# GpSimd's 512-column two-input operations issued as two of 256 columns in a two-layer transformer kernel

## The chip, the cores and the metric

The kernel runs on one core of a Trainium2 chip. The metric is the device time of one execution in microseconds; less is better. The core has five engines with a queue each: TensorE (PE, its weight loads shown as PEld), VectorE (DVE), ScalarE (ACT), GpSimd (POOL) and SyncE (SP), which here issues all DMAs.

## The reference

Two layers of a pre-norm transformer, B = 8 sequences of T = 1024 tokens, D = 256 features, 16 heads of 16. Each layer is attention and a feed-forward part, both on a layer norm of the input and both added to it:

```
x = x + L0_attn(layernorm(x))      # softmax(q k^T / 4, causal) v, then w_out
x = x + L0_ffn(layernorm(x))       # gates by entmax-1.5 over 16 experts; factorised experts with gelu
x = x + L1_attn(layernorm(x))      # low-rank q, k, v; half of each head's q and k rotated:
                                   #   x * cos + rot(x) * sin
x = x + L1_ffn(layernorm(x))       # squared-relu shared expert, and a top-2 router whose
                                   # truncated weights are 0 unless one logit dominates
```

## The kernel before

The work is cut into chunks: a sequence b, a half c of its tokens (512, one PSUM bank of columns), a layer l. An attention **pass** is (b, l, c), 32 in all; a **unit** is one of four groups of four heads in a pass. A planner written in Python (`Plan`, `program_order`) runs once before the code is emitted and gives one list, `ORDER`. Every engine walks through that list and emits its own share of each item, in order, so the order on each engine's queue is fixed and the engines meet only at semaphores.

What each item is on which engine, as far as the change matters:

- **Projection** (`qk`): TensorE makes 128 rows by 512 tokens of q or k, ScalarE copies them to a `scratch` buffer in float32 (L1581).
- In layer 1 these are **rotated**: VectorE swaps neighbouring rows (`swap_pairs`, L1865, a stream shuffle from scratch to scratch), GpSimd multiplies the original by the cosine table (`times_cos`, L1761), the swapped copy by the sine table (L1782) and adds the two (L1785, both in `rotate`).
- **Splitting**: q and k are stored as two float16 parts. ScalarE makes the first (`parts` slot 0, L1588 in layer 1, L1580 in layer 0), GpSimd subtracts it from the float32 value and so makes the second (`part2`, L1767). SyncE stores both to DRAM (L1057, L1058) and later loads them as the stacked operands `stk_q`, `stk_k` of the units (`load_stack`, L1073, L1075).
- **Scores**: TensorE makes score tiles (L1282), VectorE takes their row maxima out of PSUM (L1877 with the causal mask, L1880 without; L1885 joins the maxima of two halves), GpSimd splits the maxima into float16 parts (L1797 to L1799). TensorE makes the scores again, transposed, with the maximum subtracted (L1321); ScalarE writes the exponentials to `probs` (L1616); GpSimd zeroes what lies above the diagonal (`causal`, L1777); TensorE weighs the values (L1340).
- **Division**: the outputs of a unit go through DRAM; VectorE inverts the sums (L1889), SyncE stores and reloads the inverses, spread over rows (L1102, L1107), and GpSimd multiplies (`divide`, L1806). TensorE's output projection follows (L1259).
- **Layer norm**: VectorE takes statistics of each of 4 tiles of 128 tokens (`statistics`, L1844, L1850, L1852, L1853), GpSimd raises the variance to -1/2 and makes the shift (L1751, L1753), ScalarE normalises. The raw statistics of 4 tiles lie in a buffer `st6` with two slots: one for the first norm of layer 0 (n = 0), one for the three others.
- **Entmax and router**: long chains of small VectorE operations on 128 x 4 to 128 x 128 values in SBUF (L1913 to L1966 and L1976 to L1994), each waiting for the one before. GpSimd takes two powers for them (L1825, L1828).

In the four places of GpSimd's code that rotate, split and divide, each operation reads two operands of 128 rows by 512 columns and writes one, and its semaphore is raised at its end.

## Time and profile before

| | us |
|---|---|
| median of three runs | 2695.77 |
| lowest, highest | 2695.38, 2698.12 |
| the profiled execution | 2700.38 |
| its span in the trace | 2698.4 |
| TensorE busy in it | 2440.8 |
| VectorE busy | 2042.8 |
| ScalarE busy | 1869.6 |
| GpSimd busy | 1031.5 |

The span is from the first to the last instruction; some 2 us lie around it. All rows below come from the one profiled execution. Matmuls overlap in the array, and their ends are modelled, so TensorE's busy time is an upper reading. A row of a group gives the mean duration of one instruction and the idle time of the engine just before them with what ended it; a row of the timeline gives the start, the length and, in brackets, the idle time before.

### The profile page before, as it was taken

What the parts mean: (1) busy time and instruction counts of PE and PEld (TensorE: products, weight loads), DVE (VectorE), ACT (ScalarE), POOL (GpSimd) and SP (SyncE); (2) the same over time, 40 slices, a digit from 0 to 9 for tenths busy, and PEclk for the clock granted to TensorE, in tenths of its full rate; (3) what the DMA queues carried; (4) which work ended last, traced back from release to release, by engine and by line L of the source; (5) the groups of instructions that cost most, each with busy time, mean ns of one, the idle gap of its engine ahead of it and who ended that gap; (6) DMA issues with size and microseconds to landing.
All of it is one profiled execution on the core that took longest, in us unless ns stands there. A gap on an engine that the chain in (4) does not pass through costs nothing. (4 is left out here: it accounts for less than half of the span.)

```text
span 2698.4 us, 53735 instructions
## 1 busy us (share of the span) xinstructions
PE 2440.8 (90%) x17565; PEld 976.1 (36%) x17565; DVE 2042.8 (76%) x5616; ACT 1869.6 (69%) x3804; POOL 1031.5 (38%) x1710
## 2 busy tenths in 40 slices
PE   6889789999899998999999999999999999989785
PEld 3324233334333343333433343333433334334223
DVE  4884787967879578885888779786897868784862
ACT  3577467777677766687677777677677777856572
POOL 2324443254424363153532545244452534343221
PEclk9899899999899999999999999999999999989897
DMA  5311222224212242222421133212331222211211
GB/s 189 93 46 48 88 68 87 69 74 120 93 60 81 65 124 81 64 74 73 121 82 60 64 100 116 66 61 75 117 107 55 86 84 86 76 57 45 78 56 65
DMA packets 192482, 219.47 MB, mean 81 GB/s; under 512 B 36912, under 2 KB 143824, under 8 KB 192208
## 3 DMA queue, kind: packets, MB, share of 16 engines
q1 hardware_dynamic: 192208, 215.97, 26.1%
q8 instruction: 153, 2.51, 0.4%
q14 instruction: 121, 0.99, 0.1%
HBM read 113.07 MB, written 101.71 MB: 80 GB/s over the span
## 5 line engine op out<-in xcount | busy, mean ns | idle before, releaser
L1616 ACT ACTIVATE probs<-ps 128x512 f32<-128x512 f32 (+2 forms) x2560 | 1245.7, 560 | 465.8 <-PE ps L1321 458.6
L1880 DVE TENSOR_REDUCE mx<-ps 128x1 f32<-128x512 f32 (+2 forms) x1536 | 897.4, 638 | 233.4 <-PE ps L1282 134.0
L1877 DVE CUSTOM_DVE_ANT_0 ps<-ps,mask_b 128x512 f32<-128x512 f32 (+1 forms) x1024 | 613.7, 651 | 188.3 <-PE ps L1282 179.2
L1777 POOL TENSOR_SCALAR_AFFINE_SELECT probs<-probs 128x256 f32<-128x256 f32 (+1 forms) x768 | 368.9, 484 | 930.9 <-ACT probs L1616 927.1
L1340 PE MATMUL ps<-probs,vaug 128*17 128x512 f32 (+3 forms) x6144 | 602.3, 501 | 14.8 <-ACT probs L1616 6.1
L1282 PE MATMUL ps<-stk_k,stk_q 48*128 48x512 f16 (+3 forms) x3072 | 460.9, 336 | 87.5 <-issue 29.0
L1321 PE MATMUL ps<-stk_q,stk_k 50*128 50x512 f16 (+3 forms) x3072 | 451.5, 333 | 70.2 <-DVE mx L1877 23.1
L1321 PEld LDWEIGHTS ps<-stk_q,stk_k 50*128 50x128 f16 x3072 | 139.7, 94 | 465.8 <-issue 334.4
L1282 PEld LDWEIGHTS ps<-stk_k,stk_q 48*128 48x128 f16 x3072 | 141.7, 95 | 455.0 <-issue 322.1
L1251 PE MATMUL ps<-turned,wqkv 128*128 128x512 f32 x512 | 278.6, 640 | 8.9 <-ACT turned L1555 3.8
L1340 PEld LDWEIGHTS ps<-probs,vaug 128*17 128x17 f32 x6144 | 139.5, 97 | 293.6 <-issue 208.0
L1767 POOL TENSOR_TENSOR parts<-scratch,parts 128x512 f16<-128x512 f32 x128 | 148.2, 1158 | 108.9 <-ACT scratch L1581 86.5
L1568 ACT ACTIVATE xn<-x,shift,rstd 128x256 f32<-128x256 f32 x256 | 139.4, 603 | 44.1 <-POOL shift L1753 44.1
L1259 PE MATMUL ps<-wo,yT 128*128 128x256 f32 x512 | 145.1, 413 | 14.2 <-issue 8.6
L1877 DVE DVE_READ_ACCUMULATOR2_ANT mx<- 128x1 f32 x1024 | 144.6, 141 | 0.0
L1400 PE MATMUL ps<-ffn,win 128*128 128x512 f32 x256 | 143.1, 641 | 0.0
L1259 PE MATMUL ps<-wqkv,turned 128*128 128x256 f32 x512 | 138.1, 400 | 1.5 <-ACT probs L1616 0.8
L1894 DVE TENSOR_TENSOR x<-ps,x 128x512 f32<-128x512 f32 x128 | 87.8, 687 | 61.4 <-PE ps L1259 60.4
L1797 POOL TENSOR_SCALAR low<-mx 128x16 f32<-128x16 f32 x128 | 34.5, 269 | 257.1 <-DVE mx L1885 187.4
L1806 POOL TENSOR_TENSOR yT<-yT,inverse 128x512 f32<-128x512 f32 x64 | 81.4, 1272 | 115.1 <-DMA inverse<-inverse_sums 114.9
L1625 ACT ACTIVATE mT<-ps 8x512 f16<-8x512 f16 x128 | 73.8, 577 | 66.8 <-PE ps L1307 66.3
L1395 PE MATMUL ps<-ffn,wout1T 128*128 128x512 f32 x256 | 116.7, 608 | 2.0 <-DVE ffn L1971 1.8
(165 smaller groups left out, 2543.9 us busy)
## 6 DMA issues: line engine op xcount, KB each, us to landing
o<-oT SPq DMA_DIRECT2D x128, 256.0 KB, 2.2
stk_q<-q SPq DMA_DIRECT2D x256, 96.0 KB, 2.5
stk_k<-k SPq DMA_DIRECT2D x128, 192.0 KB, 3.6
q<-parts SPq DMA_DIRECT2D x64, 256.0 KB, 2.1
k<-parts SPq DMA_DIRECT2D x64, 256.0 KB, 2.1
yT<-o SPq DMA_DIRECT2D x64, 256.0 KB
inverse<-inverse_sums SPq DMA_DIRECT2D x64, 256.0 KB
stk_k<-k SPq DMA_DIRECT2D x128, 96.0 KB, 2.4
```

The costliest lines, as they stand in the source:

```text
L1251: ins = pe.matmul(pt, wqkv[l][:, kd, D * w + P * m:D * w + P * (m + 1)], xT(2 * l, b, c, kd), start=kd == 0, stop=kd == KD - 1)
L1259: ins = pe.matmul(pt[:, D * i:D * (i + 1)], left(kd)[:, cols], right(kd), start=kd == 0, stop=kd == n_k - 1)
L1282: ins = pe.matmul(out[:, width * a:width * (a + 1)], q, stk_k[rows, slot, h + a, BANK * p:BANK * p + width], start=a == 0, stop=a == n - 1 ...
L1321: ins = pe.matmul(out[:, width * k:width * (k + 1)], stk_k[rows, slot, h + k, P * j:P * (j + 1)], stk_q[rows, slot, h + k, cols], start=Tr ...
L1340: ins = pe.matmul(o_bank[32 * h:32 * h + DH + 1, cols], vaug[:, v, j % TPC, HG * g + h, :], probs[:, STEP[u, j] % PBUF, h, cols], start=j ...
L1400: ins = pe.matmul(acc, win2[:, k, :], hsb[k], start=k == 0, stop=k == OC - 1)
L1568: ins = act.activation(xn[:, t, :], src[:, t, :], ACT.Identity, bias=shift[:, i, t:t + 1], scale=rstd[:, i, t:t + 1])
L1616: act.activation(probs[:, step % PBUF, heads, cols], src, ACT.Exp, scale=exponent[l])\
L1767: pool.tensor_tensor(parts[:, o % PRING, 1], qf[o % QRING], parts[:, o % PRING, 0], ALU.subtract)\
L1777: pool.affine_select(out=diag, in_=diag, compare_op=ALU.is_ge, fill=0.0, base=0, pattern=[[0, k], [1, P]], channel_multiplier=-1).then_inc ...
L1877: dve.tensor_tensor_reduce(tile, tile, mask_b[:, BANK - width:BANK], 1.0, LOWEST, ALU.add, ALU.max, most)\
L1880: dve.tensor_reduce(most, tile.rearrange("q (k w) -> q k w", k=k), AX.X, ALU.max)\
```

## The change

Every two-input GpSimd operation of 512 columns (cosine, sine, sum, float16 remainder, division) becomes two of 256 columns, issued one behind the other by a helper. The first half raises no semaphore; the second raises the one that the whole operation raised. What is waited for before the first half, and the order of `ORDER`, stay as they are. GpSimd's operations on few columns and the selects of L1777 are not touched. Beside that the statistics buffer has three slots: n = 0 keeps the first, n = 1 and 2 share the second, n = 3 has the third.

```diff
+HALF_BANK = BANK // 2
@@
-        st6 = sb("st6", [P, 2, TPC, 6])
+        st6 = sb("st6", [P, 3, TPC, 6])
@@
+            def in_halves(out, one, two, op):
+                for half in range(2):
+                    cols = slice(HALF_BANK * half, HALF_BANK * (half + 1))
+                    ins = pool.tensor_tensor(out[:, cols], one[:, cols], two[:, cols], op)
+                return ins
+
             def times_cos(*key):
...
-                pool.tensor_tensor(q, q, cos[:, BANK * key[2]:BANK * (key[2] + 1)], ALU.mult).then_inc(cos_ready, 1)
+                in_halves(q, q, cos[:, BANK * key[2]:BANK * (key[2] + 1)], ALU.mult).then_inc(cos_ready, 1)
@@
             def part2(*key):
...
-                pool.tensor_tensor(parts[:, o % PRING, 1], qf[o % QRING], parts[:, o % PRING, 0], ALU.subtract)\
-                    .then_inc(parts_ready, 1)
+                in_halves(parts[:, o % PRING, 1], qf[o % QRING], parts[:, o % PRING, 0], ALU.subtract).then_inc(parts_ready, 1)
@@
-                pool.tensor_tensor(qs[w], qs[w], sin[:, BANK * key[2]:BANK * (key[2] + 1)], ALU.mult).then_inc(sin_ready, 1)
+                in_halves(qs[w], qs[w], sin[:, BANK * key[2]:BANK * (key[2] + 1)], ALU.mult).then_inc(sin_ready, 1)
                 pool.wait_ge(cos_ready, r + 1)
                 pool.wait_ge(sin_ready, r + 1)
-                pool.tensor_tensor(qf[o % QRING], qs[w], qf[o % QRING], ALU.add).then_inc(rope_ready, 1)
+                in_halves(qf[o % QRING], qs[w], qf[o % QRING], ALU.add).then_inc(rope_ready, 1)
@@
-                pool.tensor_tensor(y, y, inverse[:], ALU.mult).then_inc(y_ready, 1)
+                in_halves(y, y, inverse, ALU.mult).then_inc(y_ready, 1)
@@
             def statistics(n, c, src, tiles):
-                six = st6[:, 1 if n else 0]
+                six = st6[:, (n + 1) // 2]
```

On GpSimd's queue, at the place where the first sequence's entmax meets the first rotations of layer 1, the rows before read thus (L1806 is a division, L1828 an entmax power):

```order
L1806 TENSOR_TENSOR yT<-yT,inverse 128x512
L1782 TENSOR_TENSOR scratch<-scratch,sin 128x512
L1785 TENSOR_TENSOR scratch<-scratch 128x512
L1777 AFFINE_SELECT probs<-probs 128x2x128
L1777 AFFINE_SELECT probs<-probs 128x4x128
L1782 TENSOR_TENSOR scratch<-scratch,sin 128x512
L1785 TENSOR_TENSOR scratch<-scratch 128x512
L1828 TENSOR_TENSOR zsm<-zsm,half 128x4
```

And after, where L1759 is the helper's line and the lines below it have moved by six:

```order
L1759 TENSOR_TENSOR yT<-yT,inverse 128x256 x2
L1759 TENSOR_TENSOR scratch<-scratch,sin 128x256 x2
L1759 TENSOR_TENSOR scratch<-scratch 128x256 x2
L1783 AFFINE_SELECT probs<-probs 128x2x128
L1783 AFFINE_SELECT probs<-probs 128x4x128
L1759 TENSOR_TENSOR scratch<-scratch,sin 128x256 x2
L1759 TENSOR_TENSOR scratch<-scratch 128x256 x2
L1834 TENSOR_TENSOR zsm<-zsm,half 128x4
```

Nothing has changed its place; each operation of 512 columns stands twice with 256. VectorE's queue has the same rows as before.

## Rows read from the trace of the kernel before

**Rows 1.** The page: busy time, share of the span and instructions of each engine.

```profile
PE 2440.8 (90%) x17565; PEld 976.1 (36%) x17565; DVE 2042.8 (76%) x5616; ACT 1869.6 (69%) x3804; POOL 1031.5 (38%) x1710
```

**Rows 2.** The page: shares of the span of the chain that ended last.

```profile
PE 12%; DVE 4%; ACT 2%; issue 1%; DMA 1%; SPq 0%; POOL 0%; ACTq 0%; POOLq 0%; DVEq 0%
```

**Rows 3.** Who waited for whom: us in total, times, longest.

```profile
PEld ps L1282 <- DVE mx L1880: 38.3, 59, 1.2
...
PEld ps L1340 <- POOL probs L1777: 34.4, 92, 1.7
...
PE ps L1282 <- DMA stk_k<-k: 15.7, 6, 11.4
```

**Rows 4.** POOL's groups by form: count, busy us, mean ns, idle us before.

```profile
L1777 POOL TENSOR_SCALAR_AFFINE_SELECT probs<-probs 128x256 f32<-128x256 f32 x512 | 208.6, 409 | 701.2 <-ACT probs L1616 699.5
L1777 POOL TENSOR_SCALAR_AFFINE_SELECT probs<-probs 128x512 f32<-128x512 f32 x256 | 160.8, 635 | 229.8 <-ACT probs L1616 227.5 <-DMA inverse<-inverse_sums 1.5 <-PE ps L1282 0.2
L1767 POOL TENSOR_TENSOR parts<-scratch,parts 128x512 f16<-128x512 f32 x128 | 148.2, 1158 | 108.9 <-ACT scratch L1581 86.5 <-ACT parts L1588 22.1
L1782 POOL TENSOR_TENSOR scratch<-scratch,sin 128x512 f32<-128x512 f32 x64 | 81.6, 1275 | 0.0
...
L1799 POOL TENSOR_TENSOR mparts<-low,mparts 128x16 f16<-128x16 f32 x128 | 28.5, 222 | 10.9
```

**Rows 5.** VectorE's groups by form, four of those with small operations in SBUF.

```profile
L1852 DVE TENSOR_SCALAR minus<-mv 128x4 f32<-128x4 f32 x64 | 15.3, 240 | 2.2
L1885 DVE TENSOR_TENSOR mx<-mx 128x16 f32<-128x16 f32 x64 | 14.7, 229 | 0.4
...
L1946 DVE TENSOR_TENSOR zt<-cum 128x64 f32<-128x64 f32 x16 | 9.4, 585 | 0.6
...
L1948 DVE TENSOR_TENSOR zt<-zt,kidx 128x64 f32<-128x64 f32 x16 | 5.6, 348 | 0.6
```

**Rows 6.** Single lines of VectorE: duration ns min/median/max, first and last start.

```profile
L1885 DVE TENSOR_TENSOR mx<-mx x64: 110/168/1191, 120.1 to 2585.6; 128x16 f32<-128x16 f32 x64
...
L1946 DVE TENSOR_TENSOR zt<-cum x16: 224/226/1250, 192.4 to 2418.7; 128x64 f32<-128x64 f32 x16
...
L1988 DVE TENSOR_SCALAR zsm<-zsm x16: 169/171/999, 483.9 to 2687.0; 128x4 f32<-128x4 f32 x16
```

**Rows 7.** Timeline near 1000 us: start us, us, what, idle before.

```profile
999.63 1.27 POOL L1785 TENSOR_TENSOR scratch<-scratch 128x512 f32<-128x512 f32 x1
...
999.66 1.26 DVE L1986 TENSOR_SCALAR zsm<-zsm 128x4 f32<-128x4 f32 x1
...
1000.85 1.16 POOL L1767 TENSOR_TENSOR parts<-scratch,parts 128x512 f16<-128x512 f32 x1
...
1001.17 0.86 DVE L1988 TENSOR_SCALAR zsm<-zsm 128x4 f32<-128x4 f32 x1
...
1003.77 0.39 PE L1321 MATMUL ps<-stk_q,stk_k 50*128 50x256 f16 x4 [1.00 <-DVE mx L1880]
```

**Rows 8.** Timeline near 198 us, GpSimd and VectorE.

```profile
197.83 1.04 POOL L1828 TENSOR_TENSOR zsm<-zsm,half 128x4 f32<-128x4 f32 x1
...
198.24 0.22 DVE L1961 TENSOR_TENSOR zc<-zc,zsm 128x64 f32<-128x64 f32 x1
```

**Rows 9.** Timeline, 262 to 286 us: VectorE, SyncE and TensorE.

```profile
269.59 1.17 DVE L1917 TENSOR_TENSOR zt<-zc 128x64 f32<-128x64 f32 x1
...
279.23 0.35 DVE L1889 RECIPROCAL sums<-sums 128x32 f32<-128x32 f32 x1
...
279.61 0.32 SPq L1102 DMA_DIRECT2D inverse_sums<-sums  x1
...
284.10 1.36 PE L1282 MATMUL ps<-stk_k,stk_q 48*128 48x512 f16 x6 [11.44 <-DMA stk_k<-k]
```

**Rows 10.** Busy us of each engine in one stretch, granted clock, DMA share, GB/s.

```profile
268.00:284.10 16.10, 4.67 (x20) 3.44 (x20) 14.63 (x37) 3.57 (x6) 14.64 (x13) 0.80 0.35 104
```

**Rows 11.** Timeline near the end: the projection behind the last division.

```profile
2634.70 0.77 PE L1259 MATMUL ps<-wo,yT 128*128 128x256 f32 x1 [2.60 <-POOL yT L1806]
```

## The prediction

> **What bounds the kernel now.** I read the busy times first [rows 1]. The reader should see that TensorE has work for 2440.8 us of a 2698.4 us span, VectorE for 2042.8, ScalarE for 1869.6, and GpSimd, the only engine that the change touches, for 1031.5. Then the chain that ended last [rows 2]: where it is followed, it lies on PE for 12%, on DVE for 4%, on ACT for 2%, on DMA for 1% and on POOL for 0% of the span. GpSimd idles 701.2 and 229.8 us before its two forms of select, for ScalarE's exponentials [rows 4]. TensorE waits for GpSimd's masked probabilities only 34.4 us in 92 places [rows 3], partly behind matmuls that still drain. So GpSimd's own time is nearly free. Its effect on another engine is not: in the trace a VectorE instruction that has its operands in SBUF stops while a GpSimd operation of 512 columns runs.
>
> [rows 7] show it. DVE L1986, a TENSOR_SCALAR on 4 columns, starts at 999.66, just behind POOL L1785 (999.63, 1.27 us), and takes 1.26 us. The median of such a small operation is 0.171 us [rows 6]. The next one, L1988, is caught by POOL L1767 and takes 0.86. TensorE then idles 1.00 us for a row maximum that VectorE could not begin in time. That is where the change can gain.
>
> **The price of a split.** Two-input operations take 0.222 us for 16 columns and 1.275 us for 512 in float32 [rows 4], which is (1275 - 222) / 496 = 2.12 ns a column over a fixed 0.19 us. The form with a float16 result takes 1.158 for 512, so 1.89 ns a column. An operation of 256 columns should then take 222 + 240 x 2.12 = 731 ns, or 675 ns with float16 (estimates). The one-input select agrees that the law is straight: 0.409 us for 256 columns, 0.635 for 512, again 0.18 fixed [rows 4]. Back to back, the second operation starts before the first ends: 999.63 to 1000.85 is 1.22 us for a 1.27 us operation [rows 7], so about 0.045 of the fixed part is hidden. A pair takes 2 x 0.731 - 0.045 = 1.417 us against 1.27: **0.145 us more**, and 2 x 0.675 - 0.045 = 1.305 against 1.158 for float16, 0.147 more. Bounds for the extra are 0, if the fixed part is all hidden, and 0.28, if it is paid in full with a start of 0.09 besides. 64 operations in each of four float32 forms (L1761, L1782, L1785, L1806) and 128 of L1767 are 384 splits: 384 x 0.145 = 56 us more GpSimd time, 1031 to 1087 us. The semaphore is raised by the second half alone, so whoever waits sees 0.145 us more a step.
>
> **What of that lies on the path.** A rotated projection goes through cosine, sine, sum and float16 remainder on its way: 4 x 0.145 = 0.58 us later at the store to DRAM. Behind it stand SyncE's queue, then the stack loads, then the scores. TensorE waits for such a load in 6 places, 15.7 us in all [rows 3]. In the largest of them, 11.44 us at 284.10 [rows 9], the four loads were held at SyncE behind the store of the inverses (L1102, 279.61), which waits for VectorE's reciprocal L1889 (279.23). Only part of the six chains can thus be GpSimd's. I take two of them at 0.58. At the end of the program the division L1806 is followed at once by TensorE's output projection, which idled 2.60 us for it at 2634.70 [rows 11]: 0.15 for certain. The masks behind a split operation come 0.145 later, but few of the 92 waits stand just behind one. In all I take **1.5 us lost**, between 0.15 and the 9.3 of the slow rival.
>
> **What VectorE gets back.** Some 26 forms of 16 instructions each and two of 64 show means above their floors. L1885 has 229 ns against a median of 168: 64 x 0.061 = 3.9 us. L1852 has 240 against the 171 of L1988, which has the same form: 4.4 us. Of the forms of 16, L1946 is the worst with 585 against 226 and L1948 a middling one with 348 against the same floor [rows 5, 6]; I take 0.13 us for the average: 26 x 16 x 0.13 = 54. Together about 62 us of VectorE standing still.
>
 The five forms carry 419 / 498 = 84%, **52 us**. In halves the sum of squares is 512 x 0.54^2 + 256 x 0.485^2 = 209, half of it: 26 us would be saved with random arrivals.
>
> They are not random. In the entmax chains VectorE issues one small SBUF operation behind another. In the stretch 268 to 284.1 both engines are busy 14.6 of 16.1 us [rows 10], and there the freed operation is followed by one that meets the second half. Where both queues are dense the total time that GpSimd reads is the same and nothing is won. A lone small operation among the row maxima gains about 0.5 us. I take **16 us**, between 0 and 26.
>
> The Trainium skill speaks to this (SBUF — State Buffer, section on who interferes with whom): the port pair that the two engines share is an exclusive lock, held for the whole instruction. [rows 7] agree; [rows 8] don't, since L1961 ran inside L1828. By the rule the fixed part would be held too, the squares would be 585 before and 390 after, and a third would be saved with random arrivals, 17 us where the row's reading gives 26.
>
> What of VectorE's 16 us shortens the run? The chain that ended last is followed over 20% of the span, and 4 of these 20 are DVE [rows 2], and TensorE's weight loads wait for row maxima 38.3 us in 59 places for one pair of lines alone [rows 3], so more than a fifth may matter. I take a quarter: **4 us gained**.
>
> **The third statistics buffer** adds 96 bytes a partition and no instruction; VectorE runs its statistics in the same order with the same waits. It costs nothing, since no row here waits for that buffer but VectorE itself in its own order.
>
> **The sum.** The profiled execution took 2700.38 us (span 2698.4 and 2.0 around it). 2700.4 - 4 + 1.5 = 2697.9. The median of the three runs shown is 2695.77, 4.6 below the profiled one; the same 2.5 us off it gives **2693.3 us**, 0.1% less. A measurement of this kernel tells about 0.2% from no change, 5.4 us, so this forecast counts as the same.
>
> **The rivals.** (1) More of the standing still is on the path. For it: the stall of 1.00 us in [rows 7] follows directly from two blocked operations, and in [rows 9] the reciprocal that holds the loads stands behind blocked ones such as L1917 (1.17 us for 0.22). Against: DVE has only a fifth of the chain. If VectorE saves the full 26 us and half of it counts, 13 - 1.5 = 11.5 us go: 2684.3. Chance 0.28.
> (2) Slower: GpSimd becomes late in layer 1. Each of the 16 passes there rotates four tiles in a row; if in each the last tile's float16 parts set the stack loads and so TensorE, the 0.58 us count 16 times: 9.3 us, with nothing gained 2705.1. It decides where less than 0.58 us lie between a part's landing and the scores. Against it: only 6 waits for such loads in 32 passes. Chance 0.15.
> (3) The split does not open the door: GpSimd goes from one half to the next without letting VectorE in. Then the hold is as long as before, plus the 1.5 us lost: 2697.3. Against it: at 1000.85 POOL L1767 begins right behind L1785, and yet L1986 ends at 1000.92 [rows 7], so a waiting instruction does slip between two GpSimd operations. Chance 0.12. The Trainium skill (the same page and section) gives a lock for one instruction, which speaks against this rival as these rows do.
>
> **How the numbers follow.** The forecast has 0.45, rivals (1), (2) and (3) 0.28, 0.15 and 0.12. Faster by over 0.2% is rival (1), 0.28. The same is the forecast and rival (3), 0.57. Slower is rival (2), 0.15. For 8 in 10 the range must reach into both outer cases: from 2683, just below rival (1), to 2702, part of the way to rival (2). The predicted time is the forecast's, 2693.3.
>
> **What the profile after would show.** The five forms stand there with double counts and means near 731 and 675 ns; GpSimd is busy 1087 us, and clearly less would mean that the fixed part is hidden. The longest small VectorE operations drop from 1.26 us to about 0.75, L1946's mean from 585 to some 400 ns, L1885's and L1852's to 200. DVE's busy time falls by 16 us: if it falls by 26 and the run by over 5, rival (1) holds; if the small operations keep their maxima of 1.2 us, rival (3). TensorE's waits for stack loads grow from 15.7 us: by more than 5, and rival (2) is at work. The prediction is wrong if a pair of halves costs under 1.27 or over 1.55 us, or if DVE's saving and the run's don't go together.

## The result, and the profile after

The changed kernel took 2677.6 us (median of 6 runs, 2674.7 to 2684.9); the kernel before took 2695.8 beside it (6 runs, 2693.1 to 2700.2). The ratio is 0.9937, with a 95% interval of 0.9922 to 0.9952: 18 us less. The forecast was 2693.3 us and "the same"; the measured time lies below its range. The unaltered changed kernel, run again among the experiments, gave 0.9948 (0.9928 to 0.9969). I count its gain as 14 to 18 us.

The profiled execution of the changed kernel took 2674.7 us, with a span of 2672.7. Its busy times stand against [rows 1], and its chain that ended last against [rows 2]:

```profile
PE 2435.5 (91%) x17565; PEld 971.4 (36%) x17565; DVE 2026.5 (76%) x5616; ACT 1869.8 (70%) x3804; POOL 1084.4 (41%) x2094
```

```profile
PE 12%; DVE 4%; ACT 2%; issue 1%; DMA 0%; POOL 0%; SPq 0%; ACTq 0%; POOLq 0%; DVEq 0%
```

GpSimd is busy 52.9 us longer (1031.5 to 1084.4, and 384 instructions more), VectorE 16.3 us shorter (2042.8 to 2026.5), and the run gained about as much as VectorE did. The shares of the chain look the same as before and say nothing about the gain. One profile has a busy time only to some microseconds: the kernel before with nothing but the third statistics buffer shows VectorE at 2038.2 us, 4.6 below [rows 1], and the changed kernel run again shows 2027.3.

GpSimd's split forms (count | busy us, mean ns | idle us before, and what ended it), against [rows 4]:

```profile
L1759 POOL TENSOR_TENSOR parts<-scratch,parts 128x256 f16<-128x256 f32 x256 | 166.3, 671 | 93.9 <-ACT scratch L1582 82.2 <-ACT parts L1589 11.6
L1759 POOL TENSOR_TENSOR scratch<-scratch,sin 128x256 f32<-128x256 f32 x128 | 90.8, 730 | 0.0
...
L1759 POOL TENSOR_TENSOR yT<-yT,inverse 128x256 f32<-128x256 f32 x128 | 90.4, 727 | 108.0 <-DMA inverse<-inverse_sums 108.0
```

VectorE's small forms, against [rows 5]. Lines have moved by six, so L1946 is now L1952:

```profile
L1858 DVE TENSOR_SCALAR minus<-mv 128x4 f32<-128x4 f32 x64 | 14.1, 220 | 2.2
L1891 DVE TENSOR_TENSOR mx<-mx 128x16 f32<-128x16 f32 x64 | 13.1, 205 | 0.4
...
L1954 DVE TENSOR_TENSOR zt<-zt,kidx 128x64 f32<-128x64 f32 x16 | 7.0, 438 | 0.5
...
L1952 DVE TENSOR_TENSOR zt<-cum 128x64 f32<-128x64 f32 x16 | 5.9, 366 | 0.5
```

L1952's mean fell from 585 to 366 ns. L1954, two instructions behind it, rose from 348 to 438: a part of the blocked time has moved down the chain, as the prediction said of stretches where both queues are dense. The longest L1952 is now 762 ns (minimum/median/maximum, first and last start), where [rows 6] had 1250:

```profile
L1952 DVE TENSOR_TENSOR zt<-cum x16: 224/226/762, 191.9 to 2394.2; 128x64 f32<-128x64 f32 x16
```

**Where the time went.** The matmuls come in the same order in both traces, so the start of each can be laid beside its twin's. The lead of the changed kernel grows in steps and changes little between them: 4.7 us at 500, 7.9 at 560, 14.7 at 1080, 17.2 at 1590, 21.9 at 1735, 25.7 at the end (times of before). The step near 558 shows the mechanism, and it returns with the same size, 3.2 us, when the changed kernel's second trace is laid beside before. The trace before, in order of time (start us, us, what, idle before and its releaser):

```profile
553.40 1.16 POOL L1767 TENSOR_TENSOR parts<-scratch,parts 128x512 f16<-128x512 f32 x1
...
553.55 1.09 DVE L1957 TENSOR_TENSOR zt<-zw,zt 128x64 f32<-128x64 f32 x1
...
553.71 1.99 PE L1251 MATMUL ps<-turned,wqkv 128*128 128x512 f32 x4
...
554.51 1.26 POOL L1782 TENSOR_TENSOR scratch<-scratch,sin 128x512 f32<-128x512 f32 x1
...
554.67 0.22 DVE L1958 TENSOR_REDUCE zsm<-zt 128x4 f32<-128x64 f32 x1
...
554.80 1.05 DVE L1959 TENSOR_TENSOR zw<-zw,cum 128x64 f32<-128x64 f32 x1
...
555.92 1.26 POOL L1785 TENSOR_TENSOR scratch<-scratch 128x512 f32<-128x512 f32 x1
556.14 1.12 DVE L1961 TENSOR_TENSOR zc<-zc,zsm 128x64 f32<-128x64 f32 x1
...
557.29 1.95 DVE L1880 TENSOR_REDUCE mx<-ps 128x2 f32<-128x512 f32 x4
...
558.09 0.39 PE L1282 MATMUL ps<-stk_k,stk_q 48*128 48x512 f16 x2 [2.40 <-issue]
```

And the same instructions after:

```profile
548.06 0.23 DVE L1963 TENSOR_TENSOR zt<-zw,zt 128x64 f32<-128x64 f32 x1
...
548.46 0.31 DVE L1965 TENSOR_TENSOR zw<-zw,cum 128x64 f32<-128x64 f32 x1
...
548.66 1.30 POOL L1759 TENSOR_TENSOR parts<-scratch,parts 128x256 f16<-128x256 f32 x2
...
548.97 1.98 PE L1252 MATMUL ps<-turned,wqkv 128*128 128x512 f32 x4
549.06 0.35 DVE L1967 TENSOR_TENSOR zc<-zc,zsm 128x64 f32<-128x64 f32 x1
549.44 1.95 DVE L1886 TENSOR_REDUCE mx<-ps 128x2 f32<-128x512 f32 x4
...
550.88 0.39 PE L1283 MATMUL ps<-stk_k,stk_q 48*128 48x512 f16 x2
```

Before, each of three entmax operations ends 0.08 us after a GpSimd operation (1.09, 1.05 and 1.12 us). The reduction L1958 between them, with one input, runs in its usual 0.22 us while GpSimd's L1782 is under way. So the prediction's sentence that a VectorE instruction with its operands in SBUF stops is too wide: not every form is blocked. The row maxima L1880 are queued behind these operations on VectorE, and TensorE, whose next scores need a bank that these maxima read, idles 2.40 us. After, the three take 0.23, 0.31 and 0.35, and TensorE does not wait. The lead at the projection L1251 is 553.71 - 548.97 = 4.74 us, at the scores L1282 it is 558.09 - 550.88 = 7.21, and 7.85 one projection later. Two things are easy to miss. The wait of 2.40 us is booked as "issue", although it ends when the first row maxima are through. And not all of it is the halves: GpSimd's remainder begins 0.15 us ahead of the first of the three before, but 0.60 behind it after, so it meets fewer of them.

The prediction's own example does the same on a smaller scale. From L1986 to the row maxima behind it, VectorE took 3.37 us before (from 999.66 in [rows 7] to 1003.03) and 2.46 after (991.33 to 993.79). TensorE's wait of 1.00 us is gone, and the lead grows there by 0.91 us.

**What part of the lead is TensorE's clock.** Some steps of the lead show no such chain: every matmul in them takes longer before than after. The stretch behind 1728 is one (us, then busy us and count of PE, PEld, DVE, ACT, POOL, granted clock, DMA share, GB/s), before and after:

```profile
1728.00:1736.00 8.00, 8.00 (x30) 3.08 (x30) 3.33 (x5) 5.14 (x8) 1.27 (x1) 0.55 0.14 54
```

```profile
1709.00:1717.00 8.00, 8.00 (x38) 3.40 (x37) 4.21 (x8) 7.34 (x14) 1.41 (x2) 1.00 0.18 66
```

TensorE is busy throughout in both, but before its granted clock is 0.55, so nearly all of that time is spent at 1.2 GHz in place of 2.4. Between 1725 and 1735 the lead grows from 17.6 to 21.9 us. Just before, at 1725.20, TensorE had waited 2.01 us; after, 0.31. The stretch around 1060 looks like a second case. Before:

```profile
1062.00:1066.00 4.00, 2.92 (x20) 1.86 (x20) 3.97 (x10) 2.05 (x4) 0.00 (x0) 1.00 0.03 6
...
1070.00:1074.00 4.00, 3.57 (x14) 1.27 (x12) 4.00 (x11) 3.34 (x8) 2.32 (x7) 0.87 0.00 0
1074.00:1078.00 4.00, 3.77 (x14) 0.96 (x13) 2.36 (x6) 2.32 (x6) 0.41 (x1) 0.70 0.01 2
```

And after:

```profile
1050.00:1054.00 4.00, 3.98 (x34) 2.01 (x34) 3.97 (x11) 2.17 (x4) 0.00 (x0) 1.00 0.02 6
...
1058.00:1062.00 4.00, 3.77 (x14) 0.99 (x11) 3.73 (x11) 3.44 (x9) 1.60 (x6) 1.00 0.00 0
```

It is tempting to say that TensorE worked more and so kept its clock. The changed kernel's second trace contradicts that:

```profile
1050.00:1054.00 4.00, 3.97 (x33) 1.90 (x26) 3.97 (x11) 2.16 (x5) 0.00 (x0) 1.00 0.38 136
...
1058.00:1062.00 4.00, 3.81 (x13) 1.44 (x14) 4.00 (x10) 3.35 (x8) 2.52 (x7) 0.75 0.00 0
1062.00:1066.00 4.00, 4.00 (x9) 0.84 (x8) 1.73 (x5) 1.83 (x5) 0.41 (x1) 0.50 0.01 2
```

It has the short waits too (3.97 of 4 us), and still its clock falls to 0.75 and 0.50, lower than before the change. The lead's step near 1060, some 6 us in the first pair, is not there in this one. Over the whole run the mean clock is 0.964 before, 0.967 in the first trace of the changed kernel and 0.964 in its second. The missing part of the clock times the span, 0.036 x 2698.4, 0.033 x 2672.7 and 0.036 x 2678.6, gives 97, 88 and 96 us. So up to 9 of the first pair's 25.7 us can be the clock of that one execution (an estimate), while the second trace is 19.8 us shorter than before at the same mean clock. The gain doesn't need the clock.

### The profile page after: what moved, and what is told of

It reads as the page before. It is cut to its first block and busy times, and to the rows that moved or that the text cites. A ratio compares the mean times of both kernels' runs of the same rounds, so it can differ in the third digit from the quotient of the medians.

```text
span 2672.7 us, 54119 instructions
## 1 busy us (share of the span) xinstructions
PE 2435.5 (91%) x17565; PEld 971.4 (36%) x17565; DVE 2026.5 (76%) x5616; ACT 1869.8 (70%) x3804; POOL 1084.4 (41%) x2094
## 3 DMA queue, kind: packets, MB, share of 16 engines
q14 instruction: 125, 1.02, 0.1%
## 5 line engine op out<-in xcount | busy, mean ns | idle before, releaser
L1283 PE MATMUL ps<-stk_k,stk_q 48*128 48x512 f16 (+3 forms) x3072 | 458.9, 336 | 76.2 <-issue 18.3
L1759 POOL TENSOR_TENSOR parts<-scratch,parts 128x256 f16<-128x256 f32 x256 | 166.3, 671 | 93.9 <-ACT scratch L1582 82.2
L1260 PE MATMUL ps<-wo,yT 128*128 128x256 f32 x512 | 143.8, 409 | 12.7 <-issue 8.7
L1759 POOL TENSOR_TENSOR yT<-yT,inverse 128x256 f32<-128x256 f32 x128 | 90.4, 727 | 108.0 <-DMA inverse<-inverse_sums 108.0
```

The lines of the kernel that those rows point to most:

```text
L1260: ins = pe.matmul(pt[:, D * i:D * (i + 1)], left(kd)[:, cols], right(kd), start=kd == 0, stop=kd == n_k - 1)
L1283: ins = pe.matmul(out[:, width * a:width * (a + 1)], q, stk_k[rows, slot, h + a, BANK * p:BANK * p + width], start=a == 0, stop=a == n - 1 ...
L1759: ins = pool.tensor_tensor(out[:, cols], one[:, cols], two[:, cols], op)
```

## The experiments

All ratios are to the kernel before on the same chip, with their 95% intervals. The kernels fall into six groups by their question.

### The buffer, and two parts of the change alone

**The third statistics buffer alone:**

```diff
-        st6 = sb("st6", [P, 2, TPC, 6])
+        st6 = sb("st6", [P, 3, TPC, 6])
...
-                six = st6[:, 1 if n else 0]
+                six = st6[:, (n + 1) // 2]
```

> The kernel before with the third statistics buffer alone. Theory A (the gain is VectorE let in earlier between GpSimd's halves): no change, ratio 1.000, between 0.999 and 1.001. Rival B (the 96 bytes shift every later tensor in SBUF and some of the gain is that): ratio 0.997 or lower.

Measured: 2700.94 us against 2695.43, ratio 1.0017 (1.0000 to 1.0034). The buffer gains nothing; at most it costs 0.3%, and the changed kernel has it too.

**Halves in cosine, sine and sum alone:** against the changed kernel,

```diff
-                in_halves(parts[:, o % PRING, 1], qf[o % QRING], parts[:, o % PRING, 0], ALU.subtract).then_inc(parts_ready, 1)
+                whole(parts[:, o % PRING, 1], qf[o % QRING], parts[:, o % PRING, 0], ALU.subtract).then_inc(parts_ready, 1)
...
-                in_halves(y, y, inverse, ALU.mult).then_inc(y_ready, 1)
+                whole(y, y, inverse[:], ALU.mult).then_inc(y_ready, 1)
```

> Only cosine, sine and sum of the rotation in halves; the float16 remainder and the division whole. Theory A: the rotation's three forms caused the larger part of VectorE's standing still in the entmax stretches (three operations in a row), so half to two thirds of the 18 us: ratio 0.995 to 0.9965, DVE busy 8 to 11 us under the kernel before. Rival C (the gain comes where the division or the remainder is waited for): ratio 0.999 to 1.000.

**Halves in remainder and division alone** is the same edit on the other three calls.

> Only the float16 remainder and the division in halves; the rotation whole. Theory A: the rest of the gain, ratio 0.997 to 0.999, DVE busy 5 to 8 us under the kernel before. Rival C: most of the gain, 0.994 to 0.995.

Measured: 2688.46 us, ratio 0.9981 (0.9963 to 0.9999), and 2689.2 us, ratio 0.9976 (0.9961 to 0.9991), both against 2695.43. VectorE is busy 2033.1 and 2035.7 us, 9.7 and 7.1 below [rows 1], 16.8 together where the change has 16.3. The gains add up to 0.43% where the whole change has 0.52 to 0.63%, within the intervals. Both parts gain, and the expectation that the rotation carries half to two thirds of the gain was not met: the two can't be told apart.

### How long GpSimd holds VectorE, and by what

**The five forms without reading:** this kernel leaves out the rotation, the remainder and the division. In the place of each remainder and division GpSimd fills the result with zeros (a memset of 512 columns) and raises 4 columns to a power; in the place of cosine, sine and sum stands the power alone.

```diff
-                for half in range(2):
-                    cols = slice(HALF_BANK * half, HALF_BANK * (half + 1))
-                    ins = pool.tensor_tensor(out[:, cols], one[:, cols], two[:, cols], op)
-                return ins
+                pool.memset(out, 0.0)
+                idles.append(0)
+                return pool.tensor_tensor(idle[:, TPC * (len(idles) % 12):TPC * (len(idles) % 12 + 1)], half[:], neg_half[:], ALU.pow)
```

> Rotation, float16 remainder and division are left out: in their place GpSimd raises 4 columns to a power (about 1.03 us, reads almost nothing) and, for remainder and division, first fills the result with zeros. GpSimd's steps stay about as long as in the kernel before, but hold nothing that VectorE reads through. Theory A: nearly all 52 us of blocking by these five forms go from VectorE (DVE busy 1990 to 1995) and the run falls at least as far as in the changed kernel: ratio 0.985 to 0.993. Rival B or a gain from shifted timing alone: DVE busy falls, but the run stays at 0.997 to 1.000.

Measured: 2663.37 us against 2695.43, ratio 0.9884 (0.9860 to 0.9907). Its busy times:

```profile
PE 2431.4 (91%) x17565; PEld 970.6 (36%) x17565; DVE 1991.5 (75%) x5616; ACT 1868.6 (70%) x3804; POOL 1040.1 (39%) x1902
```

Two of VectorE's small forms, which are L1946 and L1852 in [rows 5]:

```profile
L1864 DVE TENSOR_SCALAR minus<-mv 128x4 f32<-128x4 f32 x64 | 12.6, 197 | 2.2
...
L1958 DVE TENSOR_TENSOR zt<-cum 128x64 f32<-128x64 f32 x16 | 3.7, 230 | 0.6
```

GpSimd is about as busy as before (1040.1 us), but VectorE is busy 51.3 us less, and the entmax form that took 585 ns takes 230, close to the floor of 226 in [rows 6]. That is what the five forms cost VectorE, and the prediction had 52. GpSimd's being busy is thus not what blocks. Nor, for VectorE's two-input operations, is writing many columns. The trace has 192 memsets of 512 columns, and such operations run at their usual length inside them:

```profile
539.16 0.53 POOL L1760 MEMSET parts<- 128x512 f16 x1
...
539.59 0.23 DVE L1973 TENSOR_TENSOR zc<-zc,zsm 128x64 f32<-128x64 f32 x1
```

What is left for them is the reading of many columns, as the prediction supposed. A one-input tensor_scalar is another matter: one that starts inside a memset at 267.76 takes 0.38 us in place of 0.17 and ends with it. The run falls by 32 us, 0.62 us for each of VectorE's.

**508 columns and 4:** the same number of instructions and the same extra time as halves, but nearly the old length of hold.

```diff
-                for half in range(2):
-                    cols = slice(HALF_BANK * half, HALF_BANK * (half + 1))
-                    ins = pool.tensor_tensor(out[:, cols], one[:, cols], two[:, cols], op)
-                return ins
+                cols = slice(0, BANK - 4)
+                pool.tensor_tensor(out[:, cols], one[:, cols], two[:, cols], op)
+                cols = slice(BANK - 4, BANK)
+                return pool.tensor_tensor(out[:, cols], one[:, cols], two[:, cols], op)
```

> The five forms in two operations of 508 and 4 columns: GpSimd pays the second operation's fixed part, some 0.15 us each and 56 us in all, as in the changed kernel, but holds VectorE as long as in the kernel before. Theory A: no gain, only the price of GpSimd being later: ratio 1.000 to 1.002, DVE busy 2040 to 2046. Rival E (the gain is that operations start at other moments): ratio 0.994 to 0.998.

Measured: 2705.05 us against 2701.04, ratio 1.0008 (0.9993 to 1.0024). VectorE is busy 2045.6 us, GpSimd 1086.1, as long as in the changed kernel. Two of its forms:

```profile
L1758 POOL TENSOR_TENSOR scratch<-scratch,sin 128x508 f32<-128x508 f32 x64 | 81.0, 1266 | 0.0
...
L1760 POOL TENSOR_TENSOR scratch<-scratch,sin 128x4 f32<-128x4 f32 x64 | 12.9, 201 | 0.0
```

VectorE gets nothing back and the run gains nothing: it is the length of the single hold that counts, and neither the number of instructions nor the later start of each. The same run prices what GpSimd's lateness of 0.15 us a step costs without a gain beside it: about 2 us (the interval reaches from -2 to 6).

The row without reads (L1958, 230 ns) and [rows 8], where VectorE ran in 0.22 us inside a 1.04 us power, say that a GpSimd instruction holds VectorE while it reads columns and not for its whole length. The Trainium skill (SBUF — State Buffer, section on who interferes with whom) has the lock held for the whole instruction; the 384 powers of some 1.02 us each that stood in the five forms' places don't agree with it.

**Quarters everywhere:**

```diff
-                for half in range(2):
-                    cols = slice(HALF_BANK * half, HALF_BANK * (half + 1))
+                for half in range(4):
+                    cols = slice(QUARTER * half, QUARTER * (half + 1))
```

> The five forms in four operations of 128 columns each. GpSimd busy 1084 + 384 x 2 x 0.145 = 1195 us; sum of the squares of the reading times halves again. Theory A: DVE busy another 6 to 8 us less (2019), run between 2665 and 2676, ratio 0.989 to 0.993. Rival D (GpSimd's later results now cost as much as is gained): ratio 0.993 to 0.998.

Measured: 2722.03 us against 2701.04, ratio 1.0068 (1.0049 to 1.0086): slower, and outside every range that was expected. VectorE is busy 2017.0 us, 9.5 less than with halves, and GpSimd 1191.2. A float32 operation of 128 columns takes 455 ns, where the law of the prediction gives 459. Halves gained 0.6% and quarters lose 0.7%, although VectorE profits more. Two rows of who waited for whom (us, times, longest):

```profile
ACT parts L1590 <- POOL scratch L1760: 76.9, 44, 9.4
...
PEld ps L1342 <- POOL probs L1784: 55.1, 115, 3.3
```

ScalarE waits 76.9 us for GpSimd's rotated sum, where the changed kernel has 23.3 and before had 16.2:

```profile
ACT parts L1589 <- POOL scratch L1759: 23.3, 13, 7.6
```

Lateness of GpSimd is thus the suspect, and the group on where it hurts tests it.

### What a microsecond of VectorE is worth, by place

**Entmax chains longer:** the changed kernel, with four more small reductions in each of the 16 chains.

```diff
+                    for _ in range(2):
+                        link(dve.tensor_reduce(zsm[:, 3, :], zc[:], AX.X, ALU.max))
...
+                    for _ in range(2):
+                        link(dve.tensor_reduce(zsm[:, 3, :], zc[:], AX.X, ALU.max))
```

> The changed kernel with four more small VectorE operations (a 128 x 64 reduction, some 0.22 us and 0.04 of waiting) in each of the 16 entmax chains, which use nothing that GpSimd holds: 16.6 us more for VectorE, all in entmax. The prediction's step (a quarter of VectorE's time in these places counts): 4 us longer than the changed kernel, ratio 0.995. Theory A2 (there a microsecond of VectorE is a microsecond of the run, or nearly): 12 to 17 us longer, ratio 0.998 to 1.000.

**Statistics longer:** the changed kernel, with one more small reduction behind each of the 64 layer-norm statistics.

```diff
+        spare = sb("spare", [P, 1])
...
+                link(dve.tensor_reduce(spare[:], six[:, TPC - 1, :], AX.X, ALU.max))
```

> The changed kernel with one more small VectorE operation (about 0.16 us and 0.04 of waiting) in each of the 64 statistics: some 12 us more for VectorE, spread over all layer norms. The prediction's step: 3 us longer, ratio 0.995. Theory A2 for entmax alone: also about 3 us. If VectorE's time counts fully wherever small operations stand: 10 to 12 us, ratio 0.998.

Busy times, of the first and of the second:

```profile
PE 2446.4 (91%) x17565; PEld 974.9 (36%) x17565; DVE 2040.7 (76%) x5680; ACT 1869.6 (69%) x3804; POOL 1084.0 (40%) x2094
```

```profile
PE 2451.7 (91%) x17565; PEld 974.6 (36%) x17565; DVE 2037.8 (75%) x5680; ACT 1871.2 (69%) x3804; POOL 1084.5 (40%) x2094
```

Measured, against 2701.04: 2702.95 us, ratio 1.0006 (0.9994 to 1.0019), and 2688.99, ratio 0.9945 (0.9928 to 0.9962). The profiled execution of the second took 2701.15 us, 12 above its median. The changed kernel was not in that group of runs; its ratio elsewhere is 0.9937 or 0.9948. The entmax chains' 14.2 us more of VectorE thus cost 0.58 to 0.69%, 16 to 19 us, the whole gain of the change: a microsecond or more for each of VectorE's (each added operation also brings some 0.04 us of waiting, so the chains grew by about 17). The statistics' 11.3 us cost at most 0.08%, some 2 us (up to 8 by the intervals). What a longer VectorE costs depends on where it is longer, and its sum for the run does not tell that.

### Halves where they count

**Halves near the chains alone:** the five forms are split only while an entmax chain or a router's chain is open in the order of work, 113 of the 384 splits. The other 271 stay whole.

```diff
+            near, chains = [False], set()
...
+                n = pieces()
+                for k in range(n):
+                    cols = slice(BANK // n * k, BANK // n * (k + 1))
...
+                if kind in ("logit", "route"):
+                    chains.add((kind, *key))
+                elif kind == "at":
+                    chains.discard(("logit", *key))
+                elif kind == "gate":
+                    chains.discard(("route", *key))
+                near[0] = bool(chains)
```

> Halves only for the 113 operations that stand in the program's order between the logits and the gates of an entmax or router chain; the other 271 whole. Theory A2 (the gain is in these chains): nearly the whole gain at less than a third of GpSimd's price (GpSimd busy 1048): ratio 0.993 to 0.995, DVE busy 2028 to 2032. Rival F (the gain comes as much from small operations elsewhere, in the statistics and the joined maxima): 0.997 to 0.999.

Measured: 2685.46 us against 2703.74, ratio 0.9946 (0.9928 to 0.9963).

```profile
PE 2434.2 (91%) x17565; PEld 970.8 (36%) x17565; DVE 2027.9 (76%) x5616; ACT 1869.3 (70%) x3804; POOL 1047.2 (39%) x1823
```

With 29% of the splits, and 15.7 us of GpSimd's time in place of 52.9, VectorE gets back 14.9 of 16.3 us, and the run's gain is that of the whole change within the interval. Nearly all of the gain comes from the splits beside these chains.

### Where GpSimd's lateness hurts

Three kernels with more quarters. In the first, `pieces()` gives 4 near a chain and 2 elsewhere. In the second and third the number of pieces goes by form:

```diff
-                in_halves(q, q, cos[:, BANK * key[2]:BANK * (key[2] + 1)], ALU.mult).then_inc(cos_ready, 1)
+                in_pieces(4, q, q, cos[:, BANK * key[2]:BANK * (key[2] + 1)], ALU.mult).then_inc(cos_ready, 1)
```

**Quarters near the chains, halves elsewhere:**

> Quarters for the same 113 operations, halves for the other 271. Quarters everywhere freed VectorE (2017) and cost 45 us. Theory G (GpSimd's own lateness has a steep price once rotations and masks queue, wherever it is): 113 x 0.29 = 33 us more GpSimd time in the rotations next to entmax, so 5 to 20 us over the changed kernel, ratio 0.996 to 1.001. Rival H (the price of quarters fell outside the chains): at or under the changed kernel, 0.990 to 0.994.

**Rotation in halves, remainder and division in quarters:**

> Rotation in halves, float16 remainder and division in quarters: 192 x 0.29 = 56 us of the 107 us that quarters everywhere add to GpSimd. Theory I (the price of quarters comes through ScalarE, which waits at L1588 for the rotated sum with exponentials queued behind): that wait stays near the changed kernel's 23 us, and the run loses at most 10 us, ratio 0.993 to 0.998. Rival J (GpSimd's time counts alike wherever it is spent): half of 45 us lost, 1.001 to 1.003.

**Rotation in quarters, remainder and division in halves:**

> Rotation in quarters, float16 remainder and division in halves: 192 x 0.27 = 51 us more GpSimd time, all of it in front of the rotated sum. Theory I: ScalarE's wait for the sum grows towards 77 us and most of the 45 us are lost, ratio 1.003 to 1.008. Rival J: 1.000 to 1.003.

Measured, all against 2703.74 us; the last column is how long ScalarE's parts waited for GpSimd's sum.

| kernel | median us | ratio (95%) | VectorE busy | GpSimd busy | wait for the sum: us, times |
|---|---|---|---|---|---|
| quarters near, halves elsewhere | 2686.48 | 0.9940 (0.9919 to 0.9961) | 2013.8 | 1116.3 | 34.9, 21 |
| rotation 2, rest 4 | 2687.92 | 0.9952 (0.9935 to 0.9969) | 2023.0 | 1137.8 | 31.0, 23 |
| rotation 4, rest 2 | 2707.67 | 1.0019 (1.0005 to 1.0033) | 2019.7 | 1138.1 | 63.5, 40 |

The first shows that the microsecond for a microsecond has an end: VectorE is busy 12.7 us less than in the changed kernel and the run is no faster (0.9940 against 0.9937 and 0.9948). What took the gain is not shown; the wait for the sum grew from 23.3 to 34.9 us.

The second and third have the same time on GpSimd, the third is even 3.3 us better on VectorE, and yet it is 0.67% slower, 18 us. The third's ratio alone would have fitted rival J, by which GpSimd's time counts alike wherever it is spent; the second's doesn't, and the pair decides. GpSimd's busy time is not what costs, but where it lies. The rows point to the rotated sum, which stands behind cosine, sine and addition in turn. The rows of the two, in this order:

```profile
ACT parts L1589 <- POOL scratch L1759: 31.0, 23, 8.3
```

```profile
ACT parts L1589 <- POOL scratch L1759: 63.5, 40, 9.0
```

**The sum late, with no further split:** the changed kernel with one power on 4 columns, a form that did not hold VectorE in the kernel without reads, ahead of each of the 64 sums.

```diff
+                pool.tensor_tensor(idle[:, TPC * (r % 4):TPC * (r % 4 + 1)], half[:], neg_half[:], ALU.pow)
```

> The changed kernel with one power of 4 columns (1.03 us, holds nothing that VectorE reads through) on GpSimd before each of the 64 rotated sums: 66 us more GpSimd time, all ahead of the sum, and no further split. Theory I (lateness of the sum is what quarters cost; three more fixed parts are 0.8 us a rotation there): 20 to 45 us over the changed kernel, ratio 1.001 to 1.010, ScalarE's wait for the sum 60 us or more. Rival K (the count of instructions or the finer alternation with VectorE costs): near the changed kernel, 0.993 to 0.996.

Beside it ran **the changed kernel, unaltered**:

> The changed kernel, unaltered, on the chip of these two runs. All theories: ratio 0.992 to 0.995.

Measured, against 2699.91 us: 2711.72, ratio 1.0046 (1.0030 to 1.0063), and 2685.13, ratio 0.9948 (0.9928 to 0.9969). GpSimd is busy 56.8 us longer, 0.9 us for each of the 64 places, and the run takes 26.6 us longer. Shares of the span of the chain that ended last, and the wait for the sum, in the late kernel:

```profile
PE 11%; DVE 3%; POOL 2%; ACT 2%; issue 1%; DMA 1%; SPq 0%; ACTq 0%; POOLq 0%; DVEq 0%
```

```profile
ACT parts L1590 <- POOL scratch L1760: 63.4, 40, 8.5
```

And in the unaltered one:

```profile
ACT parts L1589 <- POOL scratch L1759: 23.5, 13, 7.7
```

ScalarE's float16 part waits for the sum, with the exponentials behind it in ScalarE's queue, which TensorE needs. GpSimd, with 0% of the chain before and after, appears in it with 2% once the sum comes later. The delay alone, with no split added, costs 26.6 us. Quarters in the rotation, with about as much added GpSimd time (53.7 us), cost 19 to 22 against the changed kernel's two ratios. The wait for the sum is the same: 63.4 us in 40 places and 63.5 in 40. So lateness at this place is enough to explain what quarters lose, and neither the number of instructions nor the finer alternation with VectorE is needed.

By which way it reaches TensorE is less certain. GpSimd's masks stand in the same queue, and TensorE's waits for them grow too, from 38.0 to 46.0 us of weight loads and from 3.3 to 7.1 of matmuls between the unaltered and the late kernel. VectorE is also busy 6.0 us longer in the late one. And the rotation lies in layer 1 alone, while half of the remainders and divisions lie in layer 0, so the table doesn't tell the sum from a fuller queue of GpSimd in layer 1. No run delays the masks or the sum without the other.

### A version from both findings

**Near the chains rotation in halves, remainder and division in quarters; elsewhere whole:**

```diff
+            def rotating(*args):
+                return in_pieces(2 if near[0] else 1, *args)
+
+            def other(*args):
+                return in_pieces(4 if near[0] else 1, *args)
```

> Next to entmax and router chains the rotation in halves and remainder and division in quarters; everything whole elsewhere. Theory A2 with theory I: VectorE gains as much as in the changed kernel or some us more (DVE busy 2022 to 2028), and GpSimd's rotations are no later than there: ratio to the kernel before 0.990 to 0.994, at or 5 us under the changed kernel. Rival (the 18 us have another source): 0.996 or more.

Measured: 2677.69 us against 2699.91, ratio 0.9925 (0.9908 to 0.9942), the lowest but for the kernel without reads, with a wait for the sum of 17.7 us in 10 places. It beats the kernel before by 22 us. Against the changed kernel beside it the medians differ by 7.4 us, 0.23%, but the intervals overlap and its profiled execution was no shorter (span 2685.0 against 2678.6), so whether it beats that one stays open.

## Why the prediction was wrong

**The price of a split: right.** Predicted 0.731 and 0.675 us a half, measured 0.727 to 0.730 and 0.671; predicted 56 us more for GpSimd, measured 52.9. The law carried on to quarters too.

**The loss from a later GpSimd: right in size, wrong in place.** The forecast had 1.5 us; 508 and 4 columns showed about 2, with an interval as wide again. Its places were different from those I named. Waits for stack loads fell instead of rising, from 15.7 us in 6 places to 14.0 in 5. The projection behind the last division, where I had 0.15 us "for certain", waited 1.27 us instead of 2.60. And a row that did grow, ScalarE's wait for the rotated sum (16.2 us in 9 places before), is not in the prediction at all. With 0.145 us a step it grew to 23.3 us; with 0.9 us on the sum it is 63.4 and the run 27 us longer. The slow rival (2) had the right kind of mechanism, in the wrong place, and its 9.3 us did not come.

**VectorE's blocked time: right.** 52 us for the five forms, measured 51.3. The gain of 16 us of VectorE's busy time, measured 16.3 and, in the second trace, 15.5; the step from random arrivals' 26 down to 16 for dense chains holds, and L1954's rise shows the reason. Both closenesses are partly luck. The 16 was a choice between 0 and 26, the 52 rests on an average of 0.13 us taken for 416 operations, and profiles of kernels that hold VectorE alike differ by 4.6 us (2042.8 and 2038.2).

**The rival that the split opens no door: refuted**, by VectorE's 16.3 us and by the longest L1952, 762 ns.

**The share of it on the path: wrong, and the step that failed.** The prediction took "a quarter: 4 us gained". The change gained 14 to 18 us for VectorE's 16.3, a ratio near one. Its range ended at 2683 us because no rival let more than half of VectorE's time count, and the measured 2677.6 lies below it. The longer entmax chains gave a ratio of one or more in the other direction, the longer statistics about a fifth. So no single share exists: what the split gives back is the entmax's and the router's time (14.9 of 16.3 us came from the 113 splits near those chains), and there VectorE is what TensorE waits for.

Two readings led to the quarter. The chain that ended last is followed over a fifth of the span, the last 540 us, while most steps of the lead lie before it, near 400, 560, 1060, 1590 and 1735 us: at 2160 it is 21.7 of 25.7 us. And the waits for the row maxima in [rows 3], 38.3 us, are only those that the profile can name. The 2.40 us at 558.09 stand under "issue". The rows of that name for the scores' matmuls (us, times, longest) were, before,

```profile
PEld ps L1282 <- issue: 322.1, 568, 11.8
...
PE ps L1282 <- issue: 29.0, 61, 2.4
```

and after

```profile
PEld ps L1283 <- issue: 306.4, 556, 11.5
...
PE ps L1283 <- issue: 18.3, 47, 1.8
```

They shrank by 15.7 and 10.7 us (the two overlap), where the named rows hardly moved: L1282's loads waited 38.3 us for the row maxima before and 37.5 after. The row of the loads is a weak witness, though: it is 313.3 us in the changed kernel's second trace and 314.7 with 508 and 4 columns, which gained nothing. The row of the matmuls tells these apart (18.3 and 20.7 us in the changed kernel, 25.4 to 29.0 in three kernels without a gain), but it is 23.0 with halves near the chains alone, which have nearly the whole gain. That the unnamed waits misled the estimate is shown for the one at 558.09 and argued for the rest.

The right reading was in the prediction's own first example: in [rows 7] two blocked operations are followed by a 1.00 us wait of TensorE, and there the run gained what VectorE gained, 0.91 us. Rival (1) took it as evidence for a larger share and gave 11.5 us with half of 26; its mechanism is the one that held, with all of 16 in place of half of 26. The prediction's sign for it was VectorE down by 26 us and the run by over 5; only the second came.

**The statistics buffer: right**, no gain (1.0000 to 1.0034).

**What stays open.** How much the clock adds in an average execution is not known: the mean of one trace of the changed kernel was above that of before, that of the other the same. The two halves of the change gave 0.43% together against 0.52 to 0.63% for the whole, which the intervals allow but do not settle. And why the run without reads gave only 0.62 us for each of VectorE's 51.3 is only argued: a part of that time lies away from the chains, where a microsecond counts less. Nor is it shown why quarters near the chains, which freed VectorE by 12.7 us more, gained nothing more.

## What to carry to other kernels

When an engine's small operations are blocked by another's long ones, ask which chain they stand in and who waits at its end, and price the saved microsecond there, not by the engine's share of the chain view. If doubt remains, lengthen two stretches by a known amount and look which one moves the time. Split the long operation where such a chain runs beside it; splitting again brought nothing more here. Keep further splits away from a result that a third engine with work queued behind it waits for. And lay a second execution beside the first before a step of the lead is explained: one of 6 us didn't return.

## What the runs showed of the hardware

- A two-input GpSimd operation on many columns blocks VectorE's tensor_tensor and tensor_scalar operations in SBUF (0.22 us became 1.05 to 1.12, 0.171 became up to 1.26), but not its reductions (0.22 us at 554.67). 508 columns in one piece gave VectorE nothing back (2045.6 us busy), 256 in two pieces gave 16.3 us. Powers on 4 columns of 1.02 us each in the place of all 384, half of them behind a memset of 512 columns, gave 51.3. A memset of 512 columns left two-input operations alone (0.23 us at 539.59) and held one tensor_scalar (0.38 us at 267.76).
- A waiting VectorE operation slips between two halves issued back to back, without any wait or gap written between them: the longest L1952 fell from 1250 to 762 ns.
- Three VectorE operations of 1.1 us in place of 0.3 in one chain became a TensorE wait of 2.40 us.
- TensorE's granted clock differs between two executions of the same kernel at the same place: 1.00 from 1058 to 1066 us in one, 0.75 and 0.50 in the other, with TensorE busy 3.97 to 3.98 of 4 us from 1050 in both.
- 0.145 us more on each of four GpSimd steps cost some 2 us in all, and 0.9 us on one of them 27 us (with VectorE 6.0 us longer): the cost of being late is far from proportional.
